# One product in four by C moves from GpSimd to VectorE in a fused Mamba and ternary FFN kernel

## What is computed

```python
x_dbl = einsum('ke,bel->bkl', x_proj_w, u)          # u: conv and silu of ctx's projection
dt_lo, Bm, Cm = x_dbl[:, :16], x_dbl[:, 16:32], x_dbl[:, 32:]
delta = softplus(einsum('er,brl->bel', dt_proj_w, dt_lo) + dt_proj_b)
def step(state, xs):
    dA = exp(d_t[..., None] * A)
    state = state * dA + (d_t * u_t)[..., None] * B_t[:, None, :]
    y_t = einsum('ben,bn->be', state, C_t)
y = (y + D * u) * silu(z)
...
x = x + tanh(g_xattn) * y ; x = x + tanh(g_ffn) * ffn(layernorm(x))
```

## Time and profile before

| | |
|---|---|
| median of 3 runs | 878.03 us (876.99 to 881.62) |
| the profiled execution | 881.37 us, of which the span from first to last instruction is 879.1 us |
| VectorE busy | 780.2 us, 89% of the span, 746 instructions |
| GpSimd busy | 658.3 us, 75%, 242 instructions |
| TensorE busy | 630.7 us, 72% |
| ScalarE busy | 543.6 us, 62% |
| mean granted TensorE clock | 0.837 of full speed |
| tiles of the state-space layer | from 40 us to 780 us of the span, then the tail |

### The profile page before, as it was taken

The page is one execution under the profiler, slowest core; times in us unless marked ns, Lnnn a source line. Parts: engine busy times, 40 slices in busy tenths (PEclk is TensorE's granted clock), DMA queues, the critical chain, the costliest instruction groups (busy, mean ns, idle before and its releaser), DMA issues.

```text
span 879.1 us, 7586 instructions
## 1 busy us (share of the span) xinstructions
PE 630.7 (72%) x2354; PEld 248.4 (28%) x2354; DVE 780.2 (89%) x746; ACT 543.6 (62%) x783; POOL 658.3 (75%) x242
## 2 busy tenths in 40 slices
PE   5575655857867685878768586958686776858996
PEld 3211122323323221223223232313132222314443
DVE  2497979999999999999999999999999999968874
ACT  4586844766553765766749394746666574726773
POOL 1047776565776779796979899796979797986652
PEclk9767675988777887988879788989788787779999
DMA  3594530256320000032000000032000000000000
GB/s 92 116 333 164 214 108 12 100 155 191 132 78 18 12 1 12 0 112 60 13 8 16 0 25 0 16 107 61 12 13 12 13 12 1 12 13 13 13 25 36
DMA packets 26262, 51.25 MB, mean 58 GB/s; under 512 B 6720, under 2 KB 9280, under 8 KB 24048
## 3 DMA queue, kind: packets, MB, share of 16 engines
q1 hardware_dynamic: 26224, 50.78, 18.3%
HBM read 46.32 MB, written 4.46 MB: 58 GB/s over the span
## 4 chain that ended last, share of the span: by engine, by line
POOL 44%; DVE 29%; PE 11%; issue 11%; DMA 2%; ACT 1%; SPq 1%; DVEq 0%; POOLq 0%
POOL hb L526 14%; DVE hb L874 13%; POOL h L496 10%; POOL delta L469 7%; DVE hb L866 7%; POOL a L484 4%; DVE h L1098 3%; PE ring L1238 3%; POOL a L482 3%; PE dl_ps L1209 2%; PE du_ps L1216 2%; POOL zsc L530 2%; POOL yz L490 1%; POOL fsc L504 1%; PE ring L1290 1%
## 5 line engine op out<-in xcount | busy, mean ns | idle before, releaser
L526 POOL TENSOR_TENSOR hb<-hb,c_rep 128x2048 f32<-128x2048 f32 x64 | 294.8, 4606 | 162.1 <-DVE hb L874 147.5
L874 DVE TENSOR_TENSOR_SCAN hb<-dA,hb 128x2048 f32<-128x2048 f32 x64 | 345.2, 5393 | 4.0
L641 ACT ACTIVATE dA<-dl_ps,a_neg 128x511 f32<-128x511 f32 x256 | 154.6, 688 | 122.5 <-PE dl_ps L1209 114.1
L866 DVE TENSOR_TENSOR hb<-du_ps,b_rep 128x2048 f32<-128x2048 f32 x64 | 146.2, 2284 | 13.9 <-PE du_ps L1216 12.8
L1209 PE MATMUL dl_ps<-delta,sel_q 128*128 128x512 f32 x128 | 85.9, 759 | 101.1 <-POOL delta L469 83.7
L1227 PE MATMUL y_ps<-hb,sel_s 128*32 128x512 f32 x512 | 132.1, 663 | 11.5 <-POOL hb L526 11.5
L496 POOL TENSOR_TENSOR h<-h,g3b 128x1024 f32<-128x1024 f32 x32 | 116.6, 3645 | 21.1 <-ACT work L701 21.1
L1216 PE MATMUL du_ps<-du,sel_q 128*128 128x512 f32 x128 | 93.5, 822 | 39.4 <-DVE hb L866 36.6
L1238 PE MATMUL ring<-w1T,a12T 128*128 128x512 fp8e4 x256 | 72.5, 409 | 24.4 <-DVE delta L846 15.3
L649 ACT ACTIVATE h<-ring,deq 128x512 f32<-128x512 f32 x64 | 43.2, 680 | 57.3 <-PE ring L1238 57.0
L1238 PE MATMUL ring<-w2T,a12T 128*128 128x512 fp8e4 x256 | 70.2, 399 | 0.0
(11 more groups left out here) (130 smaller groups left out, 998.5 us busy)
## 6 DMA issues: line engine op xcount, KB each, us to landing
h<-in_L_ffn_w_dram SPq DMA_DIRECT2D x24, 1024.0 KB, 5.3
xt<-in_x_dram SPq DMA_DIRECT2D x16, 256.0 KB, 2.7
b_rep<-bc_scratch SPq DMA_DIRECT2D x16, 256.0 KB, 4.5
c_rep<-bc_scratch SPq DMA_DIRECT2D x16, 256.0 KB, 4.8
x<-in_x_dram SPq DMA_DIRECT2D x4, 1024.0 KB, 8.5
out_dram<-x SPq DMA_DIRECT2D x16, 256.0 KB, 2.0
ctx_nat<-in_ctx_dram SPq DMA_DIRECT2D x4, 512.0 KB, 5.3
g3b<-in_L_ffn_g_dram SPq DMA_DIRECT2D x1, 1024.0 KB, 12.1
```

The source lines that it names most:

```text
L526: g.tensor_tensor(hb[:, s % 4, :, :], hb[:, s % 4, :, :], c_rep[:, :, :], ALU.mult)\
L641: ins = a.activation(dA[:, s % 2, i, 1:L], dl_ps[:, 1:L], ACT.Exp, scale=a_neg[:, s % 16, i:i + 1])
L866: v.tensor_tensor(hb[:, s % 4, :, :], du_ps[:, :].unsqueeze(1).to_broadcast([P, NH, L]), b_rep[:, b % 2, :, :], ALU.mult).then_inc(dbu_don ...
L874: v.tensor_tensor_scan(flat, dA[:, s % 2, :, :].rearrange("p a l -> p (a l)"), flat, 0.0, ALU.mult, ALU.add).then_inc(scan_done, 1)
```

## The change

The product with C of step q=3 leaves GpSimd and becomes an instruction of VectorE, `mul_c`, directly behind that step's scan. GpSimd keeps q=0, 1 and 2. The products of the two engines are counted by two semaphores, `hc_done` (3 a tile) and the new `hc_dve` (1 a tile); `load_c` and the sum of steps q=2 and q=3 wait for both. `mul_c` itself waits for its scan and for C.

```diff
             def load_c(b):
                 if b >= 1:
-                    sp.wait_ge(hc_done, 16 * b)
+                    sp.wait_ge(hc_done, 12 * b)
+                    sp.wait_ge(hc_dve, 4 * b)
...
-                    pool.wait_ge(scan_done, s + 1)
-                    if s % 16 == 0:
-                        pool.wait_ge(ld_c, 64 * (b + 1))
-                    g.tensor_tensor(hb[:, s % 4, :, :], hb[:, s % 4, :, :], c_rep[:, :, :], ALU.mult)\
-                     .then_inc(hc_done, 1)
+                    if q < Q - 1:
+                        pool.wait_ge(scan_done, s + 1)
+                        if s % 16 == 0:
+                            pool.wait_ge(ld_c, 64 * (b + 1))
+                        g.tensor_tensor(hb[:, s % 4, :, :], hb[:, s % 4, :, :], c_rep[:, :, :], ALU.mult)\
+                         .then_inc(hc_done, 1)
...
+            def mul_c(s):
+
+                dve.wait_ge(scan_done, s + 1)
+                dve.wait_ge(ld_c, 64 * (s // 16 + 1))
+                v.tensor_tensor(hb[:, s % 4, :, :], hb[:, s % 4, :, :], c_rep[:, :, :], ALU.mult).then_inc(hc_dve, 1)
...
                     if q == 3:
+                        mul_c(s)
                         if ftb >= 0:
                             mul_up(ftb, 0)
...
             def sum_states(p):
 
                 k = p // 2
-                pe.wait_ge(hc_done, 2 * p + 2)
+                pe.wait_ge(hc_done, 3 * k + 2 + p % 2)
+                if p % 2 == 1:
+                    pe.wait_ge(hc_dve, k + 1)
```

More of the change, by code:

```diff
@@ L240, in flamingo_block @@
         hc_done = sem("hc_done")
+        hc_dve = sem("hc_dve")
         sum_done = sem("sum_done")
```

## The result

The changed kernel took 883.44 us (median of 8, 880.74 to 884.99), the kernel before 878.32 us on the same chip (median of 8, 876.99 to 881.62). The ratio is 1.005, with an interval of 1.0031 to 1.0068: 4.4 us slower, between 2.7 and 6.0 (the two medians by themselves lie 5.1 apart). The forecast was +2.1 us. So the sign was right, the time lies in the range, and the sum was 2.3 us short.

The account below looks back on a forecast made before the run. VectorE's queue was taken to set the pace. Ordinary boundaries +11.1, tiles 0 to 5 +0.15, earlier C -6.3 and last tile -2.85 gave +2.1 us: from 878.03 to 880.1 us, range 870 to 887.

Parts of the forecast that it names:

- What bounds the kernel, and the exclusion: VectorE's queue sets the pace; its instructions with two SBUF inputs, the new 2.28 us product included, exclude GpSimd's.
- The first rival: The new product does not exclude GpSimd, so du is in time: sum -10.3 us, 867.7 us; chance 0.12.
- Who goes first: After q=3's scan, GpSimd's waiting delta goes first, then the new product, ending at 3.21 us, before du.
- The second rival: GpSimd keeps its turn at delta's end, so the product ends at 5.54: +20.3 us, 898.3 us; chance 0.06.
- The ordinary tile: Boundaries of tiles 6 to 14, counted from S, q=3's scan end: 1.75 us later, 0.52 back, net 1.23, 11.1 for nine.
- Tiles 2 to 5: Boundary changes of +0.45, -1.9, -2.1 and +1.0 us, with instructions held up behind L526 freed in tiles 3 and 4.
- Tiles 0 and 1: VectorE waits for PE's broadcast of du, late by 1.87 us with 0.5 hidden: +1.35 us each.
- C: The next batch's C loads earlier, so tiles 8 and 12 no longer start waiting for it: -6.3 us.
- the third rival: The 6.3 us of C's wait do not come back: +8.4 us, 886.4 us; chance 0.1.
- The last tile: In tile 15 PE's last sum starts earlier, no longer behind GpSimd's last L526: -2.85 us.
- From the trace to the median: The +2.1 us sum on the profiled execution, 3.3 us above the median of 878.03, carries over: median 880.1 us.

Follow-up runs that it names:

- e5: Changed kernel, but from tile 1 on VectorE's new product takes its second factor from PSUM (y_ps), not C from SBUF: ratio 0.9891 to the kernel before.
- e4: Kernel before with the fourth product by C moved to VectorE in all tiles except 3, 7, 11 and 15: ratio 1.0141 to the kernel before.
- e6: Changed kernel with the next batch's load_c also waiting for that batch's first product with B: ratio 1.0124 to the kernel before.
- e8: Kernel before with the fourth product by C moved to VectorE only in tiles 3, 4, 7, 11 and 15: ratio 0.9891 to the kernel before.
- e9: Kernel before with extra matmuls, results unread, filling TensorE's idle time at the head and before each tile's delta broadcast: ratio 0.9976 to the kernel before.
- e12: Changed kernel with batch 1's load of C one place earlier in SP's queue, ahead of the last weight chunk: ratio 1.0038 to the kernel before.
- e1: Kernel before, unchanged, timed and traced again: ratio 0.9993 to the kernel before.
- e2: Changed kernel, unchanged, timed and traced again: ratio 1.0052 to the kernel before.
- e3: Kernel before with the fourth product by C moved to VectorE only in tiles 3, 7, 11 and 15: ratio 0.9901 to the kernel before.
- e7: Changed kernel with VectorE's new product moved to the end of q=3, behind the second mul_up: ratio 1.0106 to the kernel before.
- e10: Changed kernel with the same extra TensorE matmuls as e9: ratio 1.0051 to the kernel before.

## Why the prediction was right, and what it missed

**What bounds the kernel, and the exclusion: right, and shown.** That busy time is no cost by itself came from comparing the scan with itself. VectorE's busy time rose by 25.7 us, the time by 4.4. e5 shows the cause directly, by taking one SBUF input away. The Trainium skill, "SBUF — State Buffer", section "Who interferes with whom", which the prediction cited for the plain product, is borne out: 3.17 us with two SBUF inputs and 2.29 with one, beside the same delta. The first rival is gone for the product as it is.

**Who goes first: right.** Product before du, in all nine boundaries. The second rival's products of 5 us don't occur. In tiles 2 and 3, where GpSimd has nothing to run at that place, and in tiles 4 and 15, where it has only one-column work, the product takes 2.29 us.

**The ordinary tile: right in size.** The next product with B was put at S+6.64 and came at S+6.70; the free scan at 4.41 and came at 4.42. The six tiles that have nothing else cost 7.9 us against 7.4.

**Tiles 2 to 5: right.** The held-up instructions of the earlier trace rows are free now; from the end of tile 3:

```profile
210.49 2.29 DVE L883 TENSOR_TENSOR hb<-hb,c_rep 128x2048 f32<-128x2048 f32 x1
212.69 1.28 DVE L1108 TENSOR_SCALAR h<-h,w_inv 128x2048 f32<-128x2048 f32 x1
213.89 0.16 DVE L961 TENSOR_SCALAR at<-at 128x3 f32<-128x3 f32 x1
```

Three columns take 0.16 us, where the same instruction (L952 before) took 4.47.

**Tiles 0 and 1: too small.** +1.56 and +1.72 instead of 1.35 each. TensorE and then VectorE at the end of tile 0:

```profile
73.86 2.08 PE L1219 MATMUL dl_ps<-delta,sel_q 128*128 128x512 f32 x2 [8.68 <-POOL delta L471]
77.13 2.08 PE L1226 MATMUL du_ps<-du,sel_q 128*128 128x512 f32 x2 [1.20 <-POOL du L477]
```

```profile
79.24 2.29 DVE L869 TENSOR_TENSOR hb<-du_ps,b_rep 128x2048 f32<-128x2048 f32 x1 [3.29 <-PE du_ps L1226]
```

Du came 1.20 us after delta's broadcast had ended, and TensorE, which had waited again, took 2.08 for its own, where it had taken 1.91 behind the other without a gap. The step had carried over the old duration of a broadcast to a place where the engine now idles ahead of it. It is 0.6 us of the sum.

**C: right.** -3.84 was the net forecast for tiles 8 and 12, -3.72 came; e4, which leaves these two products on GpSimd, keeps the wait, and e6 brings it back. C lands at S+9.8 to S+10.3 in tiles 8 and 12 of the two traces, where S+10.7 was forecast, with 3.2 to 3.7 us to spare instead of 2.7. So the third rival is gone.

**The last tile: right, and a gift on top.** Timeline rows at the end of tile 15 after, VectorE and GpSimd:

```profile
777.83 6.87 DVE L877 TENSOR_TENSOR_SCAN hb<-dA,hb 128x2048 f32<-128x2048 f32 x1
784.73 2.29 DVE L883 TENSOR_TENSOR hb<-hb,c_rep 128x2048 f32<-128x2048 f32 x1
```

```profile
780.38 4.66 POOL L506 TENSOR_TENSOR fsc<-fsc,half_neg 128x1 f32<-128x1 f32 x1
785.01 2.42 POOL L502 TENSOR_TENSOR h_sc<-h_sc,half_neg 128x1 f32<-128x1 f32 x1
```

The sum starts 2.47 us behind the scan instead of 5.39, 2.92 earlier, as forecast (2.85). But it also takes 1.20 us less. The stretch of this sum, first before and then after (columns as in the earlier trace rows):

```profile
785.95:792.30 6.35, 6.35 (x16) 1.29 (x16) 0.00 (x0) 0.96 (x2) 2.44 (x2) 0.54 0.03 12
```

```profile
787.17:792.30 5.13, 5.13 (x16) 1.25 (x16) 3.80 (x9) 2.83 (x4) 2.12 (x3) 0.67 0.07 27
```

The same 16 matmuls, at a granted clock of 0.54 and of 0.67: TensorE left the lower level earlier. The prediction had no term for that. The traces of all kernels have this last sum anywhere between 4.96 us (e8) and 6.50, at 4.99 even for before with filler (e9). For one kernel it repeats: 6.50 and 6.42 in the two traces of before, 5.30 and 5.23 in those of the changed kernel, 5.18 in e12. Whether the 1.2 us belong to the change or to these executions is not shown.

**From the trace to the median: the step that was short.** The prediction made its sum on the traced execution and carried it to the median unchanged: "it lies 3.3 above the median of the three runs, 878.03, so the median becomes 880.1 us". That is only right if the changed kernel's traced execution stands to its median in the same way, and it doesn't. That of the changed kernel (880.74) was the fastest of its 8, 2.7 us below the median. Those of before were near the slowest both times (881.37 with a highest of 881.62, then 881.6).

The traces name two things that set an execution's place, both of them TensorE's clock: the head and the last sum. Before was traced with the long head and the long sum both times. By an estimate from its own traces and those of the others, with the short head (1.8 us less) and a sum of 5 us (1.4 less) the 881.6 of e1 would be 878.4, while its median is 879.3. The changed kernel was traced first with the short head and the short sum (880.74), then with the long head and the short sum (882.95, where the median is 883.3). So a good part of the 3.3 us was how before happened to be traced.

With the head left out and the last sums made equal, the traces put the changed kernel 2.8 us above before, and e2 as well. That is 0.7 over the forecast, of which 0.6 is tiles 0 and 1. The same sum for the other kernels, with the timed difference in brackets, gives -8.5 for e3 (-8.7), -9.5 for e5 (-9.6), +10.7 for e6 (+10.9), +8.6 for e7 (+9.3), -10.0 for e8 (-9.6) and +2.9 for e12 (+3.3), but +10.6 for e4 (+12.4). So the way of counting holds to within 0.8 us in six kernels, and is 1.6 to 1.8 us short in the changed kernel, its repetition and e4. This rest stays open. The intervals of the single comparisons reach down to 2.7 and 3.1, and that of e12, whose tiles are the same, to 1.8, so the noise nearly covers each; e4's ends at 10.9 and does not reach 10.6. That all three lie above 2.8 (4.4, 4.6, 3.3), and e4 above its own, fits an effect in the executions that no trace holds, but does not show one. The clock at ordinary boundaries is not it, by e9 and e10.

The chances gave 0.29 to a loss of over 0.5% and 0.52 to no measurable change. At 1.0050 and 1.0052 the result is on that border.

## What to carry to other kernels

An operation that changes between VectorE and GpSimd takes along whether it can run beside the other engine: price it by comparing one operation's durations at several places in the trace, for both engines and for those that wait behind them, and not by busy time. Here the same move cost 1.3 us in a tile where nothing waited on it and gave 2 to 4 where a buffer, a sum or a small instruction did; moving it in four or five tiles of sixteen made the kernel 1% faster, in all sixteen 0.5% slower. And a sum made on one traced execution is a sum about that execution: before a forecast of a few microseconds is carried to a median, trace the same kernel more than once and look for stretches that the change does not touch and that differ all the same. Here the head did, by 2.2 us between two traces of one kernel, as much as the whole forecast.

## What the runs showed of the hardware

- In tile 15 a waiting one-column GpSimd instruction did not hold up VectorE's product, though it was itself held up by the scan: L506 took 4.66 us behind the scan and ended 0.31 us into the product, L502 took 2.42 beside it, and the product still took its free 2.29.
- The head of the kernel, the same instructions in every trace without filler, took 38.5 to 38.9 us or 40.4 to 41.0: eight matmuls in it took 3.60 us where the granted clock between 20 and 31 us was 1.00, and 4.97 or 5.30 where it was 0.84.
- The same 16 matmuls (behind 7.25 us of idle time in after, 9.28 in before, 9.10 in e9) took 4.96 to 6.50 us over all kernels, and within 0.12 us the same in the traces of one kernel.
- Ten matmul passes that end 3.1 us before a broadcast left it at the lower level in tile 10 of e9 (2.07 us for two passes) and not in tile 13 (1.12).
- At an ordinary boundary of the kernel before, the higher level brought VectorE's next product 0.16 us forward, and the scan behind it, against the same GpSimd instruction, took 0.17 longer.
